# A mixture-of-experts block: down matrices loaded from SP's queue in the order of use, the last shared add one group earlier, the last pair's token rows in front of its gate

## What is computed

```python
logits = xf @ w_router.T                    # xf: layer norm of x2, 2048 x 512
top_vals, top_idx = jax.lax.top_k(logits, 4)   # of 64 experts
w_tok = softmax(top_vals)
# each expert e takes its first C = 64 (token, slot) pairs, x_ec = xf[tok_ec]
g = silu(einsum('ech,ehi->eci', x_ec, w_gate))      # w_gate, w_up: 64 x 512 x 384
u = einsum('ech,ehi->eci', x_ec, w_up)
y = einsum('eci,eih->ech', g * u, w_down)           # w_down: 64 x 384 x 512
combined = zeros.at[tok_ec].add(y * w_ec)           # scatter-add to the tokens
combined += (silu(xf @ w_sh_gate) * (xf @ w_sh_up)) @ w_sh_down   # shared expert
out = x2 + combined
```

## Time and profile before

| | |
|---|---|
| median of 3 runs | 752.04 us (750.35 to 753.28) |
| the profiled execution's own time | 751.08 us |
| its span, first to last instruction | 749.0 us |
| mean granted TensorE clock | 0.964 of full speed |
| TensorE busy | 694.9 us, 93% of the span |
| VectorE / ScalarE / GpSimd busy | 327.3 / 151.4 / 225.3 us |
| DMA | 203.35 MB, 271 GB/s over the span |

### The profile page before, as it was taken

The page is one execution under the profiler, slowest core; times in us unless marked ns, Lnnn a source line. Parts: engine busy times, 40 slices in busy tenths (PEclk is TensorE's granted clock), DMA queues, the critical chain, the costliest instruction groups (busy, mean ns, idle before and its releaser), DMA issues. The chain is left out here.

```text
span 749.0 us, 9947 instructions
## 1 busy us (share of the span) xinstructions
PE 694.9 (93%) x3229; PEld 439.8 (59%) x3229; DVE 327.3 (44%) x839; ACT 151.4 (20%) x244; POOL 225.3 (30%) x234
## 2 busy tenths in 40 slices
PE   2999999699999898999999999999999999999881
PEld 1799988598997864445445445445445445444330
DVE  5887569838877683322322322322322322323130
ACT  5722214313120221112112112112112112112010
POOL 5537455315546413020321221203321220203111
PEclk9999999589999879999999999999999999999896
DMA  8101007500009997999999999999999999999953
GB/s 322 51 14 43 1 15 241 208 15 1 14 1 360 412 410 243 363 379 395 380 365 391 356 385 381 390 349 380 394 385 385 350 386 386 388 350 386 389 155 41
DMA packets 78883, 203.35 MB, mean 271 GB/s; under 512 B 9299, under 2 KB 9427, under 8 KB 78336
## 3 DMA queue, kind: packets, MB, share of 16 engines
q1 hardware_dynamic: 46592, 123.89, 43.2%
q10 hardware_dynamic: 23184, 57.42, 19.6%
q0 software_dynamic: 9072, 21.59, 12.3%
HBM read 178.92 MB, written 24.12 MB: 271 GB/s over the span
## 5 line engine op out<-in xcount | busy, mean ns | idle before, releaser
L1503 PE MATMUL bank<-w_sb,xT 128*64 128x384 f32 x1024 | 175.0, 495 | 6.7 <-DMA w_sb<-in_L_ffn_w_up 5.9
L582 POOL DMA_INDIRECT out_dram<-ym,midx x32 | 51.4, 1605 | 294.6 <-issue 143.1
L1503 PEld LDWEIGHTS bank<-w_sb,xT 128*64 128x64 f32 x1024 | 71.2, 138 | 92.7 <-issue 80.7
L1142 DVE TENSOR_TENSOR gu<-sg,bank 128x384 f32<-128x384 f32 x48 | 26.6, 554 | 194.5 <-issue 156.7
L1521 PE MATMUL bank<-w_sb,guT 128*64 128x512 f32 x384 | 87.9, 593 | 0.7 <-DVE ym L1195 0.7
L1424 PE MATMUL bank<-sh_sb,xS 128*128 128x384 f32 x208 | 69.2, 486 | 0.0
L1147 DVE COPY guT<-bank 128x384 f32<-128x384 f32 x45 | 23.9, 555 | 78.1 <-PE bank L1511 75.6
L1521 PEld LDWEIGHTS bank<-w_sb,guT 128*64 128x64 f32 x384 | 27.7, 138 | 48.6 <-issue 48.6
L800 ACT ACTIVATE sg<-bank 128x384 f32<-128x384 f32 x48 | 23.5, 490 | 161.5 <-PE bank L1503 110.4
L1424 PEld LDWEIGHTS bank<-sh_sb,xS 128*128 128x128 f32 x208 | 38.7, 191 | 24.1
L813 ACT ACTIVATE y<-bank 128x512 f32<-128x512 f32 x32 | 19.1, 597 | 158.3 <-PE bank L1521 158.3
(11 more groups left out here) (182 smaller groups left out, 1196.3 us busy)
## 6 DMA issues: line engine op xcount, KB each, us to landing
w_sb<-in_L_ffn_w_gate SPq DMA_DIRECT2D x128, 384.0 KB
w_sb<-in_L_ffn_w_up SPq DMA_DIRECT2D x128, 384.0 KB
w_sb<-in_L_ffn_w_down ACTq DMA_DIRECT2D x116, 384.0 KB
w_sb<-in_L_ffn_w_down SPq DMA_DIRECT2D x12, 384.0 KB
ring<-in_L_attn_x SPq DMA_DIRECT2D x14, 256.0 KB, 3.4
xS<-xt_dram SPq DMA_DIRECT2D x13, 256.0 KB
xt_dram<-xwT ACTq DMA_DIRECT2D x12, 256.0 KB, 3.7
out_dram<-yS POOLq DMA_DIRECT2D x4, 768.0 KB
```

Source lines behind the costliest of these rows:

```text
L582: pool.indirect_dma_start(out=out[:, :], out_offset=bass.IndirectOffsetOnAxis(ap=midx[r][u][:, :], axis=0), in_=ym[u][:, :], in_offset=Non ...
L1142: dve.tensor_tensor(gu[n][:, :], sg[n][:, :], ps_u[u][:, 0:I], ALU.mult).then_inc(gu_ready[n], 1)
L1503: ins = pe.matmul(ps[e * C:(e + 1) * C, 0:I], xT[u][:, c, e * C:(e + 1) * C], gate_up(r, u, e, w)[:, c, :], start=(c == 0), stop=(c == KC ...
```

## The change

There are three parts. SP loads the down matrices too, at their place in the order of use: D(j,0) after U(j,1), and D(j,1) after U(j+1,0); ScalarE issues none. The last shared tile is added between the two pairs of group 14 and no more in group 15. In group 15 the token row of pair 1 is broadcast right behind that of pair 0, in front of `gate_and_up(1)`, and `same` and `midx` of pair 1 are made there; for this TensorE waits for `same` of pair 0 before it overwrites the row.

```diff
--- before.py
+++ after.py
@@ -227,6 +227,8 @@
 
             if isinstance(j, int) and j == 0:
                 return (1 + u) * ADD
+            if isinstance(j, int) and j >= GROUPS - 2:
+                return (j * 2 + (1 + u) + 4 + (j == GROUPS - 1 or u == 1)) * ADD
             return (j * 2 + (thirds + (1 - (r == 0) if u == 0 else 2))) * ADD
 
         def landed_before(j, thirds, r, u):
@@ -421,14 +423,17 @@
                     if k == 0 and shared:
                         load_shared_tile(j - 1, (r + 2) % 3)
 
-            def group(j, r, last=False, shared=True):
+            def group(j, r, last=False, shared=True, first=False):
                 for k in range(2):
                     load_matrix(j, r, 1, k)
+                if not first:
+                    load_matrix(j, r, 0, 2)
                 if not last:
                     load_even_pair(j + 1, (r + 1) % 3, shared=shared)
+                load_matrix(j, r, 1, 2)
 
             for j in range(1, 3):
-                group(j, j, shared=False)
+                group(j, j, shared=False, first=j == 1)
             with sp.Fori(0, (SHARED - 4) // 3) as i:
                 for n in range(3):
                     group(i * 3 + (n + 3), n)
@@ -586,13 +591,14 @@
                                             compute_op=ALU.add).then_inc(added, ADD)
 
                 add_pair(0, 0 if isinstance(j, int) and j == 0 else landed_before(j, thirds, r, 1))
-                batch = r == 0 and not (isinstance(j, int) and j == 0)
+                rest = isinstance(j, int) and j == GROUPS - 2
+                batch = rest or r == 0 and not (isinstance(j, int) and j in (0, GROUPS - 1))
                 if batch:
-                    tiles = 1 if isinstance(j, int) and j == GROUPS - 1 else 3
+                    tiles, t = (1, SHARED - 1) if rest else (3, j - 3)
                     pool.wait_ge(yS_ready, TOKENS // P if tiles == 1 else j + LEAD)
                     pool.wait_ge(added, landed(j, thirds, r, 0))
                     pool.nop(nofuse=True)
-                    pool.dma_start(out[bass.ds((j - 3) * P, tiles * P), :].rearrange("(a p) m -> p a m", p=P),
+                    pool.dma_start(out[bass.ds(t * P, tiles * P), :].rearrange("(a p) m -> p a m", p=P),
                                    yS[:, 0:tiles, :], accum_op=ALU.add).then_inc(added, ADD)
                 add_pair(1, landed(j, thirds, r, 0) + ADD * batch)
 
@@ -816,8 +822,6 @@
                 if not first:
                     pair_out(j - 1, 1)
                 turned_tokens(j, 1)
-                if not (first or last):
-                    fill_matrix(act, j + 1, (r + 1) % 3, 0, 2)
                 if shared:
                     silu(j + (LEAD - 1), 2, 1)
                 if first:
@@ -826,7 +830,6 @@
                 pair_out(j, 0)
                 if not last:
                     turned_tokens(j + 1, 0)
-                    fill_matrix(act, j + 1, (r + 1) % 3, 1, 2)
                 else:
                     pair_out(j, 1)
                 if shared:
@@ -1204,7 +1207,7 @@
                 dve.tensor_scalar(same[u][:, :], ps_tok[:, :], tok_col[u][:, :], wcol[r][u][:, :],
                                   ALU.is_equal, ALU.mult).then_inc(same_ready[u], 1)
 
-            def group(j, thirds, r, shared=True, first=False):
+            def group(j, thirds, r, shared=True, first=False, last=False):
                 def columns(u):
                     need(dve, same_ready[u], j)
                     dve.tensor_copy(tok_col[u][:, :], pair_tok[:, bass.ds(j * 2 + u, 1)]).then_inc(tok_col_ready[u], 1)
@@ -1224,13 +1227,17 @@
                     merged_out(j - 1, thirds - (r == 0), (r + 2) % 3, 1)
                 dve.wait_ge(tok_col_ready[0], j + 1)
                 same_tokens(j, r, 0)
+                if last:
+                    dve.wait_ge(tok_col_ready[1], j + 1)
+                    same_tokens(j, r, 1)
                 gated(j, 1, 0)
                 turn_copy(j, 1, ps_ht)
                 if shared and not first:
                     turn_copy(j + (LEAD - 1), 2, ps_d[1])
                 merged_out(j, thirds, r, 0)
-                dve.wait_ge(tok_col_ready[1], j + 1)
-                same_tokens(j, r, 1)
+                if not last:
+                    dve.wait_ge(tok_col_ready[1], j + 1)
+                    same_tokens(j, r, 1)
 
             before = seq.n
             for j in range(3):
@@ -1243,7 +1250,7 @@
                     group(i * 3 + (n + 3), i + 1, n)
             seq.base, seq.n = 0, before + per * (SHARED - 4)
             for j in range(SHARED - 1, GROUPS):
-                group(j, j // 3, j % 3, shared=j <= SHARED)
+                group(j, j // 3, j % 3, shared=j <= SHARED, last=j == GROUPS - 1)
             merged_out(GROUPS - 1, (GROUPS - 1) // 3, (GROUPS - 1) % 3, 1)
 
 
@@ -1477,7 +1484,10 @@
 
             def turn_tokens_of_pair(j, u):
                 pe.wait_ge(tok_col_ready[u], j + 1)
-                pe.wait_ge(guT_ready[u], j + 1)
+                if isinstance(j, int) and j == GROUPS - 1 and u == 1:
+                    pe.wait_ge(same_ready[0], j + 1)
+                else:
+                    pe.wait_ge(guT_ready[u], j + 1)
                 pe.matmul(ps_tok[:, :], tok_col[u][:, :].to_broadcast([P, P]), ident[:, :],
                           start=True, stop=True).then_inc(tok_row_ready[u], 1)
 
@@ -1507,6 +1517,8 @@
                 def turn_gated(n):
                     pe.wait_ge(gu_ready[n], j + 1)
                     need(pe, same_ready[1 - n], j + n)
+                    if last and n == 1:
+                        pe.wait_ge(same_ready[1], j + 1)
                     for c in range(IC):
                         ins = pe.transpose(ps_ht[:, c * P:(c + 1) * P], chunk(gu[n][:, :], c, IC), ident[:, :])
                     ins.then_inc(gu_turned[n], 1)
@@ -1535,6 +1547,8 @@
                 if not first:
                     merge_pair(j - 1, 1)
                 turn_tokens_of_pair(j, 0)
+                if last:
+                    turn_tokens_of_pair(j, 1)
                 gate_and_up(1)
                 down_pair(j, thirds, r, 0)
                 turn_gated(1)
@@ -1545,8 +1559,9 @@
                 merge_pair(j, 0)
                 if shared and not first:
                     down_shared(j + (LEAD - 1))
-                turn_tokens_of_pair(j, 1)
-                if last:
+                if not last:
+                    turn_tokens_of_pair(j, 1)
+                else:
                     down_pair(j, thirds, r, 1)
                     merge_pair(j, 1)
```

## The result

The changed kernel took 742.99 us (median of 4 runs, 739.02 to 746.26), the kernel before 751.54 us (4 runs, 750.35 to 753.28). The ratio is 0.9882, with a 95% interval of 0.9843 to 0.9920: 8.6 us faster, where 6.1 were forecast against 752.04. The profiled execution took 746.26 us with a span of 743.1.

What follows compares the result with a forecast made beforehand. TensorE (93% busy) and full DMA engines bound the kernel, POOL's add chain its end. Last add at 734.1 + 8.8 = 742.9 us span, plus 2.08 is 745.0, by the median 746.0 us; range 740.5 to 749.5.

Steps and rivals of the forecast that it cites:

- TensorE's waits: At U(14,1) and U(15,1): both waits and the slow clock go, 8.3 us on TensorE; D(15,0) is late next.
- The token rows: In front of G(15,1): a stall of some 2.2 us, paid instead of a DMA wait; no gain at the end.
- The chain: POOL's successive output additions, each waiting for the one before to land: they decide the end, (15,1) at 734.1 us.
- a loaded link: One add in POOL's chain beside full weight traffic: 9.23 us, against 5.98 us without that traffic.
- the quicker adds: Rival on POOL: with one weight queue fewer, links fall towards 5.98 us and TensorE decides; 741.1 us, chance 0.27.
- the rival: The same rival as the quicker adds: loaded links lose up to 3.25 us; 741.1 us, chance 0.27.
- What the add's move is worth: Last shared add moved from the tail into POOL's tight chain: worth little, half a microsecond beside the load order alone.
- The order did cure the wait: Answers a rival at U(14,1): late for amount of bytes, not order, so TensorE keeps its times; 748.7 us, chance 0.10.
- lateness: Rival at D(15,0): weights some microseconds later, one to one beyond 4.8 us; 750.0 us at 4 beyond, chance 0.08.
- The slower rival: Weight loads from 297 us on: one queue feeds the engines less well; 762 us with 5% less rate, chance 0.05.

Runs made afterwards that it cites:

- e5: Changed kernel, but SP issues D(j,0) behind U(j+1,0) instead of behind U(j,1); 752.59 us, ratio 1.0004 to the kernel before.
- e3: Changed kernel without its third part, the last pair's token row being broadcast at the end of group 15 again; 742.64 us, ratio 0.9888 to the kernel before.
- e4: Kernel before with only the last pair's token rows moved in front of its gate; 751.54 us, ratio 1.0002.
- e8: Changed kernel with D(15,0) loaded and multiplied in front of G(15,1) and the last shared add in group 13; 740.47 us, ratio 0.9838 to the kernel before.
- e9: e8 plus four matmuls that nothing reads, around the last transposes; 743.14 us, ratio 0.9878 to the kernel before.
- e1: Kernel before with only the down matrices moved to SP's queue in order of use; last shared add and token rows as before; ratio 0.9941.
- e6: Changed kernel, but ScalarE issues D(j,1) again and SP D(j,0); one run, 747.44 us.

## Why the prediction was right, and where it was not

**TensorE's waits: right.** U(14,1) and U(15,1) no longer wait and the clock holds; what was late next was D(15,0), as forecast. Counted from (12,0), it was to land at 717.1 - 650.25 = 66.9 us and started at 68.0. e5 shows that the order does this: with one queue and D(j,0) two matrices later all of the gain is gone.

**The token rows: right as far as measured.** 2.3 us of stall where 2.2 were worked out, paid instead of a wait for weights (e3), and no gain to be seen at the end (e4).

**The chain: the step that failed is the length of a loaded link, and with it what holds the last adds.** The forecast left (13,1) where it was, 45.4 us after (12,0), and took 9.23 us for an add beside one queue as beside two; it gave the quicker adds a chance of 0.27. Measured, (13,1) came 40.6 us after (12,0): 3.67 us less in the batch's link, 1.01 and 0.93 less in the adds around it, 0.86 more in the last link, where VectorE began its copy of the product of (13,1) only at 692.64, 1.72 us before the add, so that the product held it. The two links that the chain alone held in the changed kernel took 8.16 and 7.83 us, those of e8 and e9 8.2 to 9.2. So an add beside one queue of weights loses up to 1.4 us and mostly less than 1, not the whole 3.25 of the rival, and the 768 KB batch 3.7. The prediction set aside the shorter link because links look alike soon after ScalarE's issue and at other times. They do not stand apart in its rows: the two that it compared begin at 676.81 and 686.39, and ScalarE issues at 675.73 and 688.30, beside both.

With that, (14,0) was held by its product, 50.4 us after (12,0) instead of the forecast 54.7, and so was (15,0), where the forecast had the chain five microseconds behind its product. TensorE decides at (15,0), as in the rival, and D(15,0), at 68.0 us, with it. (15,1) came 80.6 us after (12,0); the forecast has 83.9, the rival 79.1. The time, 742.99 us, lies between the forecast's 746.0 and the rival's 741.1, nearer to the rival. That the forecast was only 3 us off is in part luck: it had the wrong thing last, but chain and TensorE lie close together.

**What the add's move is worth: wrong.** I put it at 0.5 us once the order is changed. The tails give 94.83 - 90.12 = 4.7 us (e1 to e3), nearly the full link of 4.8, and the timed ratios 0.5%. Some 1.4 us of the 4.7 is the slow D(15,0) of e1, which is not the add's doing; without it 3.3 us are left, an estimate. The reasoning was sound for a chain that is tight from (13,1) on. It became loose: with short links (14,0) and (14,1) waited for their products in e1, 14.87 us passed there between (14,1) and (15,0), and the inserted add filled that room. The product of (15,0) was ready as early as in e1 (73.8 us after (12,0) to its copy in both), and its add came 0.7 us later (75.3 us in e1, 76.0 in e3), the 0.67 us of the table above. The two parts add up: 3.9 and 4.1 us alone, 8.6 together. The recorded 743.4 us for the order alone begins with (15,0) at 723.8, a time that is not worked out; by the prediction's own links the chain would be there at 695.62 + 3 x 9.23 = 723.3.

**The other rivals.** The order did cure the wait: U(14,1) has none. Of lateness there is 1.1 us at D(15,0), 68.0 against 66.9, which the product of (15,0) passed on.

**The slower rival** has little for it: one queue moved 372 GB/s from 640 to 680 and 378 from 700 to 710, the two of before 373 and 382, and the product that hung on the last weights came earlier. (The 412 GB/s that the prediction read as SP's alone may hold more: ScalarE had issued two stores at 252.64 and 253.02, whose like took 8.1 and 10.5 us at the median to land.)

What stays open is why the first 650 us scatter by some 3 us between executions of the same code, and what the 0.67 us are; neither was tried.

## What to carry to other kernels

Look at transfers that are issued by two engines for what each is needed for, and when: here, where the DMA engines were full, the second queue delivered its load early at the expense of what was needed first, and it lengthened the additions of a third queue as well. A chain of transfers that wait for one another has loaded and unloaded links; take the length of each from a row with the same queues at work, and redo the sum when the change removes a queue. A distance between two starts is the length of a link only where the second was not waiting for its data; compare the time from the data to the start over several runs. And before calling a moved link worthless, ask which links of the chain are held by their data: there it is hidden.

## What the runs showed of the hardware

With a third queue at work, at the same total rate, the additions took longer: the 768 KB batch 15.4 to 16.6 us against 12.7 to 13.0. The Trainium skill ("DMA: Bandwidth & Descriptors", Queues, rings and completion order) says that an engine takes its queues in turn; e6 agrees, with links of 10.1 us (long, for an add) and 12.8 us (short, for the batch) side by side in one execution. The Trainium skill ("DMA: Bandwidth & Descriptors", Issuing engines are not separate DMA queues) also says that a second issuing engine only saves issue time; this holds here for the rate, 372 against 373 GB/s, and not for the latency of the others.

The granted clock went to its lower level, 1.2 GHz, after an idle TensorE of 4.3 us (before), after waits of 0.93 and 2.19 us with one product between (e1), and after 2 us at 35% (e8), and stayed up through the waits of 1.80 and 1.61 us of e3 and the 1.86 and 1.27 us of the changed kernel. The last wait alone does not decide it: 2.14 us in e6 and 2.85 us in e5 left the clock up, 5.02 us in e5 did not. In these runs a fall cost the next product 1.4 to 2.5 us. A late matrix has this second price, and so has a bubble near the end.
